# Second edge stage of a graph layer: a tile's two best experts are found inside the loop of chunks

## The reference, cut to what matters

```
x = x + gnn(xn) + mix(xn)
y = layernorm(x)
gate_logits = y @ gate_w + gate_b            # 6250 x 16
topk_vals, topk_idx = top_k(gate_logits, 2)
topk_w = softmax(topk_vals)
moe = sum_k topk_w[k] * expert[topk_idx[k]](y)
x = x + layernorm(y + moe) * gamma + beta
```

## Time and profile before

| what | value |
|---|---|
| time, median of 3 runs | 2814.59 us (2810.1 to 2815.09) |
| the profiled execution's own time | 2810.95 us |
| its span, first to last instruction | 2809.0 us |
| PE, PEld, DVE, ACT, POOL busy | 78%, 62%, 65%, 33%, 66% of the span |
| granted TensorE clock, mean | 0.939 of full speed |

### The profile page before, as it was taken

The page is one execution under the profiler, slowest core; times in us unless marked ns, Lnnn a source line. Parts: engine busy times, 40 slices in busy tenths (PEclk is TensorE's granted clock), DMA queues, the critical chain, the costliest instruction groups (busy, mean ns, idle before and its releaser), DMA issues. The chain is left out here.

```text
span 2809.0 us, 54426 instructions
## 1 busy us (share of the span) xinstructions
PE 2204.9 (78%) x11643; PEld 1733.5 (62%) x11644; DVE 1825.2 (65%) x4373; ACT 932.2 (33%) x2266; POOL 1864.1 (66%) x1942
## 2 busy tenths in 40 slices
PE   4638777777778777658888888888888479999986
PEld 3426555555555555446666666666666269999975
DVE  4767777777777777476666666666666565555546
ACT  3403333333333333202222222222222144444436
POOL 1447777777777777467777777777777126666654
PEclk9869999999999999879999999999999689999998
DMA  5535555555555555376565655565656345565546
GB/s 184 171 97 149 146 145 146 146 146 146 146 145 146 146 147 143 79 225 161 157 164 156 163 154 164 157 161 156 163 153 160 90 128 101 103 104 105 101 85 189
DMA packets 262987, 402.24 MB, mean 143 GB/s; under 512 B 78879, under 2 KB 175542, under 8 KB 262904
## 3 DMA queue, kind: packets, MB, share of 16 engines
q0 software_dynamic: 102880, 254.96, 36.8%
q1 hardware_dynamic: 122376, 105.98, 13.9%
q10 hardware_dynamic: 37663, 40.56, 4.4%
HBM read 347.09 MB, written 54.62 MB: 143 GB/s over the span
## 5 line engine op out<-in xcount | busy, mean ns | idle before, releaser
L957 POOL DMA_INDIRECT gathered<-table,idx x1568 | 1488.1, 949 | 495.5 <-issue 453.6
L1288 PE MATMUL psA_e<-scaled,hotf 128*128 128x260 f32 x3136 | 746.5, 392 | 44.0 <-issue 39.4
L1288 PEld LDWEIGHTS psA_e<-scaled,hotf 128*128 128x128 f32 x3136 | 589.4, 193 | 131.8 <-issue 48.2
L1159 ACT ACTIVATE scaled<-t_e 128x32 f32<-128x32 f32 x196 | 45.0, 230 | 733.8 <-DVE t_e L1021 722.9
L1691 POOL DMA_INDIRECT moe_d<-xscaled,xtarget x113 | 179.2, 1586 | 124.5 <-DVE xtarget L1635 52.0
L1032 DVE TENSOR_TENSOR scaled<-gathered,psDW_e 128x2048 f32<-128x2048 f32 x98 | 223.6, 2282 | 25.4 <-ACT psDW_e L1160 25.4
L1025 DVE TENSOR_TENSOR hotf<-psA_e,code_r 128x1024 f32<-128x1024 f32 x196 | 239.7, 1223 | 0.1
L1032 DVE TENSOR_TENSOR scaled<-gathered,psW_e 128x2048 f32<-128x2048 f32 x98 | 223.6, 2282 | 22.4 <-ACT psW_e L1160 22.4
L1663 PEld LDWEIGHTS xpsH<-xxT,w1e 128*128 128x128 f32 x1808 | 220.6, 193 | 6.1 <-ACT xxT L1592 0.4
L1672 PE MATMUL xpsO<-w,hidT 128*128 x904 | 216.8, 383 | 7.7 <-DVE hidT L1624 6.9
L1663 PE MATMUL xpsH<-xxT,w1e 128*128 128x128 f32 x1808 | 221.3, 276 | 0.0
(11 more groups left out here) (322 smaller groups left out, 3381.2 us busy)
## 6 DMA issues: line engine op xcount, KB each, us to landing
w<-codes_d SPq DMA_DIRECT2D x196, 256.0 KB
gathered<-table,idx POOLq DMA_INDIRECT x1592
w<-in_L_ffn_w ACTq DMA_DIRECT2D x8, 2048.0 KB, 19.1
xb<-in_L_ffn_b SPq DMA_DIRECT2D x113, 128.0 KB
table<-acc POOLq DMA_DIRECT2D x49, 130.0 KB
table<-acc ACTq DMA_DIRECT2D x49, 130.0 KB
xnT_d<-w SPq DMA_DIRECT2D x49, 128.0 KB, 2.5
w<-xnT_d SPq DMA_DIRECT2D x49, 128.0 KB, 3.8
```

The lines of the kernel that those rows point to most:

```text
L957: pool.indirect_dma_start(out=G[:, q, k, :], out_offset=None, in_=table, in_offset=bass.IndirectOffsetOnAxis(ap=idx[:, q, k:k + 1], axis=0 ...
L1159: act.activation(scaled[:, par, :, C:GW], t[:], ACT.Exp).then_inc(s["weights"], 1)
L1288: ins = pe.matmul(psA[:, q, 0:GW], hotf[:, q, k, :], scaled[:, par, k, :], start=(k == 0), stop=(k == KT - 1))
```

## The change

DVE gets a step `best` with offset 14 at the end of its list. For one tile it does what the block behind the loop did for all: bias, greatest value, its number, mask, greatest value again, its number. It has 11 chained instructions on 16 values per partition (or down to one), and two copies of two values into `top` and `which`. It waits for the tile's logits, which ACT's step `gates` (offset 13) writes one turn earlier. Behind the loop there remain the two comparisons that make the one-hot pairs for `order`. No DMA is added or removed, and no other engine's list is changed; `next_pass` stays where it stood, between the loop's last turn and the block behind it.

```diff
+            best_l, best_h = sb("best_l", [P, NX]), sb("best_h", [P, NX])
+            best_top, best_which = sb("best_top", [P, 2]), sb("best_which", [P, 2])
...
+                found = Chain(dve, s["best_steps"])
+
+                def best(t, i, b, use):
+                    found.at(t * 11)
+                    dve.wait_ge(s["gate_logits"], t + 2)
+                    found.link(dve.tensor_tensor(best_l[:], logits[:, ds(i, 1), :].rearrange("p o e -> p (o e)"), gbias, ALU.add))
+                    for k in range(2):
+                        found.link(dve.tensor_reduce(best_top[:, k:k + 1], best_l[:], AX.X, ALU.max))
+                        found.link(dve.tensor_scalar(best_h[:], best_l[:], best_top[:, k:k + 1], float(NX), ALU.not_equal, ALU.mult))
+                        found.link(dve.tensor_tensor(best_h[:], best_h[:], number[:], ALU.add))
+                        found.link(dve.tensor_reduce(best_which[:, k:k + 1], best_h[:], AX.X, ALU.min))
+                        if k == 0:
+                            found.link(dve.tensor_scalar(best_h[:], number[:], best_which[:, 0:1], -3e38, ALU.is_equal, ALU.mult))
+                            found.link(dve.tensor_tensor(best_l[:], best_l[:], best_h[:], ALU.add))
+                    dve.tensor_copy(top[:, ds(i, 1), :].rearrange("p o k -> p (o k)"), best_top[:]).then_inc(s["best_kept"], 1)
+                    dve.tensor_copy(which[:, ds(i, 1), :].rearrange("p o k -> p (o k)"), best_which[:]).then_inc(s["best_kept"], 1)
...
-                rounds = chunks(dve, both_new(dve), next_pass, (1, edge_logits), (1, placed), (8, scales, True), (1, edge_scale), (-1, one_hot), (2, own_terms), (3, gain), (5, denominators, True), (7, stats, True), (7, with_beta, True))
-
-                hold(dve, s["gate_logits"], rounds * NT + 1, s["tick"])
-                steps.link(dve.tensor_tensor(logits, logits, gbias.rearrange("p (t e) -> p t e", t=1).to_broadcast([P, NT, NX]), ALU.add))
+                rounds = chunks(dve, both_new(dve), next_pass, (1, edge_logits), (1, placed), (8, scales, True), (1, edge_scale), (-1, one_hot), (2, own_terms), (3, gain), (5, denominators, True), (7, stats, True), (7, with_beta, True), (14, best, True))
+
+                hold(dve, s["best_kept"], rounds * (2 * NT), s["tick"])
                 wide = number[:].rearrange("p (t e) -> p t e", t=1).to_broadcast([P, NT, NX])
                 for k in range(2):
-
-                    l = masked if k else logits
-                    h = pair_hot[:, :, k, :]
-                    steps.link(dve.tensor_reduce(top[:, :, k], l, AX.X, ALU.max))
-                    steps.link(dve.tensor_tensor(h, l, top[:, :, k:k + 1].to_broadcast([P, NT, NX]), ALU.not_equal))
-                    steps.link(dve.scalar_tensor_tensor(h, h, float(NX), wide, ALU.mult, ALU.add))
-                    steps.link(dve.tensor_reduce(which[:, :, k], h, AX.X, ALU.min))
-                    steps.link(dve.tensor_tensor(h, wide, which[:, :, k:k + 1].to_broadcast([P, NT, NX]), ALU.is_equal))
-                    if k == 0:
-                        steps.link(dve.scalar_tensor_tensor(masked, h, -3e38, logits, ALU.mult, ALU.add))
-
+                    steps.link(dve.tensor_tensor(pair_hot[:, :, k, :], wide, which[:, :, k:k + 1].to_broadcast([P, NT, NX]), ALU.is_equal))
```

More of the change, by code:

```diff
@@ L837, in gat_edges @@
             st, mv, rs = part(6), part(2), part(3)
-            masked = hotf[:].rearrange("p q k f -> p (q k f)")[:, 0:NT * NX].rearrange("p (t e) -> p t e", e=NX)
             number_i = sb("number_i", [P, NX], I32)
@@ L852, in gat_edges @@
             names += ["x_in0", "x_in1", "x_in2", "mixed", "halves", "moments", "yb", "root", "inverse", "scale", "xf", "stored", "xfT", "gated",
-                      "gate_logits", "number", "gap", "exp", "bias"]
+                      "gate_logits", "best_steps", "best_kept", "number", "gap", "exp", "bias"]
         s = {n: sem(f"g{layer}_{n}") for n in names}
```

## The result

The changed kernel takes 2899.74 us (median of 4 runs, 2896.91 to 2904.5) against 2814.84 us of the kernel before (4 runs beside it, 2810.1 to 2818.03): a ratio of 1.0305 (95%: 1.0284 to 1.0325), 85 us slower. The forecast was 2842 with a range of 2817 to 2872. The direction was right, and the loop slowed in the way that was forecast, but a second and larger cost came on top, the one that stands among the rivals with a chance of 0.14. The profiled execution took 2898.69 us, its span is 2896.7, 87.7 more than before.

A forecast was written before the change was run, and what follows sets the result against it. POOL's gathers were taken to set the pace, until `best` made DVE the pacemaker. 2810.95 + 32.8 (loop) - 3.1 (end) = 2840.6 us against the profiled execution, 2844.3 against the median; stated as 2842, range 2817 to 2872.

The forecast's parts named there:

- the one that stands among the rivals with a chance of 0.14: DVE's longer loop body is loaded again each round, 23 to 47 us more: 2865 to 2889 us, chance 0.14.
- the bound and the threshold: Second edge stage's loop: POOL sets the pace at 20.04 us a tile; DVE can take 1.88 us a tile free.
- the price of the step: `best` on DVE costs 2.70 us a tile, 11 links at 0.21 us plus copies and address work; bounds 2.15 to 3.2.
- The tile's period: In the loop DVE becomes the pacemaker, 0.82 us a tile more than POOL leaves: 20.86 us a tile.
- 32.8 was the term: Loop's loss: 41 x 0.82 = 33.6 us, less 0.80 us caught up in the last two chunks.
- the end: Last scale to `gap`: four `best` steps, `next_pass`, loop's end and two comparisons take 14.5 us instead of 17.63, 3.1 saved.
- 0.3 was assumed: The loop's end, between `next_pass` and the comparisons, which no row shows uncovered: 0.3 us, between 0 and 1.
- the place of the code loads in the sum: Loop body grows from 231 rows to 315; code loads got no term in the sum, only a rival.

The follow-up runs named there:

- the kernel at 0: Changed kernel with DVE's loop body in the second edge stage placed at the start of a block of 256 instructions: 2842.94 us, ratio 1.0124.
- half of it: Changed kernel, body placed at a block's start, only the first of two searches in the loop, the second behind it for all tiles: 2813.14 us, ratio 1.001.
- at 160: Changed kernel with DVE's loop body started 160 instructions into a block, ending at 504: 2850.18 us, one run.
- padded by 12: Changed kernel, body not placed, with 12 semaphore increments on DVE ahead of the second edge stage's loop: 2843.97 us, one run.
- 176: Changed kernel with DVE's loop body started 176 instructions into a block, ending at 520: 2896.04 us, one run.
- 200: Changed kernel with DVE's loop body started 200 instructions into a block, reaching into a third block: 2878.49 us, ratio 1.0243.
- 239: Changed kernel with DVE's loop body started 239 instructions into a block, ending at 583: 2890.26 us, one run.
- the body of 510 at 0: Kernel before, its DVE loop body holding twelve turns instead of six (510 instructions), placed at a block's start: 2821.87 us, ratio 0.9997.
- the padding of 120: Changed kernel, body not placed, with 120 semaphore increments on DVE ahead of the second edge stage's loop: 2886.74 us, one run.
- the hint: Changed kernel with a hint to the engine that the loop's end branches back, instead of a place: 2847.8 us, one run.

## Why the prediction missed

**Right: the bound and the threshold.** POOL led, DVE had 1.88 us a tile to spare, and more than that turns the order round. The whole step in the kernel at 0 (some 2.85 us) and half of it (some 1.5) lie on the two sides of that number and behaved so; no run lies nearer to it. The gather waits are gone, POOL waits for `scaled`.

**Right within its bounds: the price of the step**, 2.70 us. In the loop it took 2.62 to 3.04 us from its first link to `both_e`, mostly about 2.87. One turn, 2.90 us long (`both_e` at 1723.22), its first links:

```profile
1720.32 0.17 DVE L1125 TENSOR_TENSOR best_l<-w 128x16 f32<-128x16 f32 x1
1720.52 0.17 DVE L1127 TENSOR_REDUCE best_top<-best_l 128x1 f32<-128x16 f32 x1
1720.72 0.23 DVE L1128 TENSOR_SCALAR best_h<-best_l,best_top 128x16 f32<-128x16 f32 x1
1720.99 0.18 DVE L1129 TENSOR_TENSOR best_h<-best_h,number 128x16 f32<-128x16 f32 x1
1721.20 0.17 DVE L1130 TENSOR_REDUCE best_which<-best_h 128x1 f32<-128x16 f32 x1
1721.41 0.38 DVE L1132 TENSOR_SCALAR best_h<-number,best_which 128x16 f32<-128x16 f32 x1
```

The plain links are as the earlier trace rows had them, 0.17 long and 0.21 apart. What was too low is the three TENSOR_SCALAR, whose operand is a value per partition: 0.23 to 0.45 us, on average 0.25. The tile's period was forecast at 20.86 and came to 21.01. In the kernel at 0 the last `z_e` starts 37.1 us later than before, where 32.8 was the term; up to 2.74 us of it are the single stop at its loop's first instruction. The two kernels without any stop, at 160 and padded by 12, agree better still: from first to last `z_e` they take 33.2 and 32.9 us more than before.

**Right: the end.** Scale to `gap` was priced at 14.5 us and took 14.42 (2294.01 + 0.16 to 2308.59):

```profile
2294.01 0.16 DVE L1119 SCALAR_TENSOR_TENSOR w<-w 128x1 f32<-128x1 f32 x1
2294.08 0.17 DVE L1125 TENSOR_TENSOR best_l<-w 128x16 f32<-128x16 f32 x1
...
2304.76 0.22 DVE L1068 MEMSET psW_e<- 128x196 f32 x1
...
2306.57 1.98 DVE L1144 TENSOR_TENSOR w1e<-number,which 128x784 f32<-128x784 f32 x2 [0.50 <-DVE window_tile L1074]
2308.59 0.21 DVE L1145 TENSOR_TENSOR gap<-top 128x49 f32<-128x49 f32 x1
```

The four steps take 10.6 us without a wait between them, the first right behind the scale; between `next_pass` and the comparisons 0.50 us are idle, where 0.3 was assumed; the steps of the three tiles ahead of them lie under a wait for `psY` that still took 4.39 us where it was 3.90.

**Wrong: the place of the code loads in the sum.** "The code loads are the one thing that no sum shows" is the step that failed. The sum took them as nothing, and they were 52.3 us in the loop. They are most of the miss: the profiled execution came 58.1 us above the sum's 2840.6, which is 52.3 for the stops, 1.8 for the rest of the loop (34.6, not 32.8) and 5.0 behind `gap`, less 1.1 at the end (4.2, not 3.1). The mechanism was named, but as a rival at 0.14, and its price, "a small load's way, 1.8 us as for `idx`", was too low: a stop is 2.7 to 3.6 us, and in this kernel a second one of 1.3 to 1.7 follows it, together 4.7 us in each of 12 rounds and not 1.8 to 3.6 in 13; its 2865 to 2889 therefore stayed below the 2899.74. The chance, too, could have been worked out. By the rule of the Trainium skill a body of up to 257 instructions fits into two blocks wherever its head falls, and before, the body of six turns has about half of the 510 that twelve turns have, some 255. The rule thus gives no loads before, as the trace shows, and is no comfort for 344: they fit only if the head falls into the first 169 places of a block (512 - 344 = 168), and in the other 87 of 256 the loads come in each round. An estimate by that rule is one in three and not 0.14; the condition is borne out by the placed kernels at 0, 160, 176, 200 and 239, but not by the body of 510 at 0 nor by the padding of 120. The likeliest case would have stayed the same, but the range would have had to reach over the loads' case. The prediction counted rows of the order (315) and not instructions of the program (344).

**What stays open:** why 510 instructions with their head at 0, which fit by the rule, still had stops; why 120 instructions of padding gave a stop, and whether the second stop is the load of the next block; and the 5.0 us behind `gap`, which lie within what that part varies by between the kernels at 0 and 200. The placed kernels show that the stops hang on the place of the body; for the unplaced one the padding makes it likely, but does not say where the head lay.

## What to carry to other kernels

Before work goes into a loop, find which engine leads it and what the follower has to spare per round: here 1.88 us a tile were free, and what went beyond was paid, first by the work and then by any stop that the spare time had covered until then. Count the instructions of the loop's body in the engine's program, not the rows: where it can outgrow what the engine keeps, the price is a stop in each round, and whether it is paid depends on the body's place, so fix the place (or try the hint, of which there is one run), and look for instruction packets in the steady part of the DMA queues. Work for all tiles that need not be in the loop goes cheaper into the waits of the drain than into the rounds, one long instruction for 43 tiles (0.87 us) instead of 43 short ones (0.17 to 0.45 each).

## What the runs showed of the hardware

- A round of DVE's loop that has to load its code stops for 2.7 to 3.6 us at its first instruction; with a body of 344 instructions the change comes between an end at 504 (no stop, 2850.18 us) and at 520 (12 stops, 2896.04 us).
- Twelve increments of a semaphore ahead of a loop made a kernel 56 us faster (2899.74 to 2843.97), most likely since they moved its body. With the place alone changed (0 and 200) it is 35.6 us, 1.2%: timings of edits in front of a loop can be off by that much.
- TENSOR_SCALAR on 16 values with a per-partition operand that the instruction before has written took 0.23 to 0.45 us, in the median 0.23; the TENSOR_TENSOR and TENSOR_REDUCE on 16 values beside it took 0.17, seldom up to 0.25. Which feature of it costs the more was not tried.
- A semaphore increment in DVE's own program is not free: 120 of them left DVE idle for 11.58 us and 200 for 19.33, 0.1 us each.
